# First attention sets loaded during the projection, and the norm sums one step later

## The reference, cut to what matters

```python
h = _layernorm(x, axis=-1) * (1 + ca) + sa
q = rmsnorm(proj(wq_w, wq_b), qn_w)
k = rmsnorm(proj(wk_w, wk_b), kn_w)
v = proj(wv_w, wv_b)
allowed = (i[None, :] <= i[:, None]) & (i[:, None] - i[None, :] < WINDOW)
scores = jnp.einsum('bhqd,bhkd->bhqk', q, k) * scale
attn = jax.nn.softmax(jnp.where(allowed[None, None], scores, -jnp.inf), axis=-1)
out = jnp.einsum('bhqk,bhkd->bhqd', attn, v)
...
def _wn(v, g):                 # the experts' weight norm: a sum of squares over each row
    n = jnp.sqrt(jnp.sum(v * v, axis=-1, keepdims=True))
    return v / jnp.maximum(n, EPS) * g[:, None]
```

## Time and profile before

| what | value |
|---|---|
| median of 3 runs | 2500.89 us (2485.25 to 2501.75) |
| profiled execution, its own time | 2496.8 us |
| its span | 2494.9 us |
| PE busy | 1932.4 us, 77% |
| DVE busy | 1669.4 us, 67% |
| ACT busy | 1089.1 us, 44% |
| POOL busy | 820.3 us, 33% |
| mean granted clock | 0.87 |
| DMA of SP's and ACT's queues | 205.50 MB, 33% of 16 engines' span |

### The profile page before, as it was taken

The page is one execution under the profiler, slowest core; times in us unless marked ns, Lnnn a source line. Parts: engine busy times, 40 slices in busy tenths (PEclk is TensorE's granted clock), DMA queues, the critical chain, the costliest instruction groups (busy, mean ns, idle before and its releaser), DMA issues. The chain is left out here.

```text
span 2494.9 us, 46728 instructions
## 1 busy us (share of the span) xinstructions
PE 1932.4 (77%) x15652; PEld 1349.0 (54%) x15652; DVE 1669.4 (67%) x3311; ACT 1089.1 (44%) x2227; POOL 820.3 (33%) x692
## 2 busy tenths in 40 slices
PE   5994888976638999998199599999998724289991
PEld 2773666755537899987054233333333523177771
DVE  3664566646778666665589587888774577765555
ACT  2772444443526333332166066666566344232222
POOL 1454333430234333332067211111111033356650
PEclk8996999987559999999599599999999855599996
DMA  4337988822336211111535824444420101242226
GB/s 142 127 138 159 183 161 169 171 67 86 129 108 191 91 52 48 48 52 35 201 138 180 147 45 69 69 69 69 69 36 2 30 32 64 94 125 84 82 77 223
DMA packets 176821, 253.47 MB, mean 102 GB/s; under 512 B 29380, under 2 KB 118500, under 8 KB 174564
## 3 DMA queue, kind: packets, MB, share of 16 engines
q1 hardware_dynamic: 157124, 205.50, 33.0%
q0 software_dynamic: 14976, 40.91, 5.3%
q10 hardware_dynamic: 4512, 4.24, 0.5%
HBM read 170.59 MB, written 79.21 MB: 100 GB/s over the span
## 5 line engine op out<-in xcount | busy, mean ns | idle before, releaser
L848 DVE TENSOR_REDUCE a_mx<-a_pmx 128x1 f32<-128x512 f32 (+5 forms) x928 | 506.0, 589 | 184.9 <-PE a_pmx L714 80.9
L912 ACT ACTIVATE a_probs<-a_pst 128x512 f32<-128x512 f32 (+2 forms) x864 | 426.0, 552 | 359.4 <-PE a_pst L732 194.9
L709 PE MATMUL a_pmx<-a_Ks,a_Qs 96*128 96x192 bf16 (+4 forms) x1280 | 344.9, 309 | 64.0 <-DMA a_V<-v_d 62.7
L1841 PE MATMUL m_ph<-m_zh,m_w 128*128 128x256 f16 x2808 | 327.9, 277 | 37.5 <-DVE m_w L1216 18.3
L1841 PEld LDWEIGHTS m_ph<-m_zh,m_w 128*128 x2808 | 274.0, 99 | 86.0 <-issue 50.1
L1857 PE MATMUL m_py<-m_w,m_zh 128*128 x2808 | 319.2, 273 | 0.6 <-DVE m_free L1907 0.4
L732 PE MATMUL a_pst<-a_Qs,a_Ks 99*128 99x192 bf16 (+5 forms) x1344 | 306.8, 291 | 9.3 <-ACT a_probs L912 6.1
L1857 PEld LDWEIGHTS m_py<-m_w,m_zh 128*128 128x128 f16 x2808 | 271.0, 98 | 32.0 <-issue 1.3
L1887 ACT ACTIVATE x_res<-m_ph,m_b,m_s 128x256 f32<-128x256 f32 x312 | 159.2, 561 | 247.3 <-PE m_ph L1841 239.3
L709 PEld LDWEIGHTS a_pmx<-a_Ks,a_Qs 96*128 96x128 bf16 x1280 | 125.1, 100 | 238.2 <-DVE a_mx L848 128.1
L1794 POOL DMA_INDIRECT m_zh<-z_d,m_src x156 | 171.2, 1098 | 225.5 <-PE m_pt L1824 182.9
(11 more groups left out here) (281 smaller groups left out, 3260.7 us busy)
## 6 DMA issues: line engine op xcount, KB each, us to landing
parts_d<-p_part SPq DMA_DIRECT2D x64, 384.0 KB, 3.2
a_Qs<-parts_d SPq DMA_DIRECT2D x192, 128.0 KB, 4.5
a_Ks<-parts_d SPq DMA_DIRECT2D x192, 128.0 KB, 7.2
v_d<-p_vt SPq DMA_DIRECT2D x16, 1024.0 KB, 4.4
a_V<-v_d SPq DMA_DIRECT2D x32, 512.0 KB, 9.1
m_got<-y_d SPq DMA_DIRECT2D x32, 512.0 KB, 6.6
a_wst<-L_w1T SPq DMA_DIRECT2D x16, 512.0 KB, 6.4
a_wst<-L_w2T SPq DMA_DIRECT2D x16, 512.0 KB, 4.9
```

Source lines behind the costliest of these rows:

```text
L709: mm = nc.tensor.matmul(pmx[:, buf, o:o + cols], Qs[par][0:KROWS, h, i * P:(i + 1) * P], Ks[par][0:KROWS, h, k0:k1], start=True, stop=not ...
L848: nc.vector.tensor_reduce(mx[:, part, hs[0]:hs[0] + len(hs), i], src, AX.X, ALU.max).then_inc(m_done, 1)
L912: nc.scalar.activation(probs[:, (hg * NV + v) % 2, hs[0]:hs[0] + len(hs), q0:q1], src, ACT.Exp, scale=HD ** -0.5).then_inc(exp_done, 1)
L1841: mm = nc.tensor.matmul(ph[:, (G * par + g) % 4, q * ROWS:(q + 1) * ROWS], self.w1[:, bass.ds(e, 1), c, wp, m * P:(m + 1) * P].rearrange(" ...
```

## The change

The 4 sets and their semaphores are made before project, so that SP can load the sets 0, 1 and 2 in slots k = 1, 3 and 5 of the projection's last batch, each after that slot's own store, in both layers. The loads at the start of attend go. In attend SP issues load_weights ahead of send_max instead of behind it. DVE's turn of expert e moves from step 2e + 1 to step 2e + 2, ahead of the same score units 3 and 6; that of the last expert goes to step 15, ahead of score units 11 and 13 of 15. POOL waits for its own four memsets before it goes on.

```diff
                     with ExitStack() as hold:
+                        self.Ks, self.Qs, self.V4 = sets("Ks", ...), sets("Qs", ...), sets("V4", ...)
+                        self.kq_in = [self.sem(hold, f"{T}kq_in{i}") for i in range(SETS)]
+                        self.project(layer)
                         self.attend(layer)
...
+            EARLY = (1, 3, 5)
...
                             sp.dma_start(pd[:, q % QK, :, ...], part[:, q % 4, :, :]).then_inc(part_out[q % 4], 16)
+                        if isinstance(b, int) and b == B - 1 and k in EARLY:
+                            if k == EARLY[0]:
+                                for half in range(2):
+                                    sp.wait_ge(v_out[half], 16)
+                                for i in range(4):
+                                    sp.wait_ge(part_out[i], 16 * 2)
+                            self.load_set(sp, layer, EARLY.index(k), 0, EARLY.index(k))
...
+            turn_at = {("st", 2 * e + 2, a): (e, a // 6) for e in range(EXPERTS - 1) for a in (3, 6)}
+            turn_at.update({("st", STEPS - 1, NE - 4): (EXPERTS - 1, 0), ("st", STEPS - 1, NE - 2): (EXPERTS - 1, 1)})
...
-                    if NORM and s % 2 and kind == "st" and a in (3, 6):
-                        dve_turn(dve, s // 2, a // 6)
+                    if NORM and (kind, s, a) in turn_at:
+                        dve_turn(dve, *turn_at[kind, s, a])
...
                         pool.memset(Ks[i][KROWS:KAUG, :, :], 1.0).then_inc(ones_set, 1)
+                    pool.wait_ge(ones_set, SETS)
...
-                    for hg in range(SETS - 1):
-                        if hg > 0:
-                            sp.wait_ge(kq_in[hg - 1], 16 * loads)
-                        load(sp, hg, 0, hg)
...
-                            send_max(sp, (hg + 1) % SETS, s + 1)
                             if NORM:
                                 load_weights(sp, 2 * b + hg // 2, hg % 2, s)
+                            send_max(sp, (hg + 1) % SETS, s + 1)
...
                     for s in range(STEPS - SETS, STEPS):
+                        if NORM:
+                            load_weights(sp, s // 2, s % 2, s)
                         if s < STEPS - 1:
                             send_max(sp, (s + 1) % SETS, s + 1)
-                        if NORM:
-                            load_weights(sp, s // 2, s % 2, s)
```

More of the change, by code:

```diff
@@ L38 @@
 HALF = 512
+SETS = 4
+LOADS = 2 * SLOTS + 1
+SLOT_Q, SLOT_K = (0, 0, 0, 1, 1, 2), (0, 1, 2, 0, 1, 0)
 HT = HALF // P
@@ L104, in build @@
             for layer in range(LAYERS):
-                self.project(layer)
                 with ExitStack() as scales:
@@ L110, in build @@
                     with ExitStack() as hold:
+                        T = f"a{layer}_"
+                        sets = lambda n, shape, t: [self.sb(hold, f"{T}{n}{i}", shape, t) for i in range(SETS)]
+                        self.Ks, self.Qs, self.V4 = sets("Ks", [KAUG, HG, L], BF16), sets("Qs", [KAUG, HG, L], BF16), sets("V4", [P, TPB, HG, 2 * HD], F32)
+                        self.kq_in = [self.sem(hold, f"{T}kq_in{i}") for i in range(SETS)]
+                        self.project(layer)
                         self.attn = self.sb(hold, f"attn{layer}", [P, TILES, D])
@@ L612, in key_blocks, with load_set @@
         return out
+    def load_set(self, sp, layer, par, b, hg):
+        pd = self.parts_d[layer]
+        row = lambda base: bass.ds(hg * (HG * HD) + base, HG * HD)
+        for dst, base, slots in ((self.Qs[par], 0, SLOT_Q), (self.Ks[par], D, SLOT_K)):
+            for s, part in enumerate(slots):
+                src = pd[part, row(base), bass.ds(b * L, L)].rearrange("(g e) n -> e g n", e=HD)
+                sp.dma_start(dst[s * HD:(s + 1) * HD, :, :], src).then_inc(self.kq_in[par], 16)
+        vsrc = self.v_d[layer][bass.ds(b * L, L), bass.ds(hg * (HG * 2 * HD), HG * 2 * HD)].rearrange("(t p) n -> p t n", p=P)
+        sp.dma_start(self.V4[par][:, :, :, :].rearrange("p t h e -> p t (h e)"), vsrc).then_inc(self.kq_in[par], 16)
     def attend(self, layer):
@@ L617, in attend @@
             T = f"a{layer}_"
-            SETS = 4
             sb = lambda n, s, t=F32: self.sb(ctx, T + n, s, t)
             sem = lambda n: self.sem(ctx, T + n)
-            Ks = [sb(f"Ks{i}", [KAUG, HG, L], BF16) for i in range(SETS)]
-            Qs = [sb(f"Qs{i}", [KAUG, HG, L], BF16) for i in range(SETS)]
-            V4 = [sb(f"V4{i}", [P, TPB, HG, 2 * HD]) for i in range(SETS)]
+            Ks, Qs, V4, kq_in = self.Ks, self.Qs, self.V4, self.kq_in
             probs = sb("probs", [P, 2, HG, HALF])
@@ L637, in attend @@
             ones_set = sem("ones_set")
-            kq_in = [sem(f"kq_in{i}") for i in range(SETS)]
             max_in = [sem(f"max_in{i}") for i in range(SETS)]
@@ L671, in attend @@
             mask = self.causal if layer else self.window
[L672 to L684, removed]
+            loads = LOADS
+            load = lambda sp, par, b, hg: self.load_set(sp, layer, par, b, hg)
             def load_weights(sp, e, second, s):
```

## The result

The changed kernel takes 2530.08 us (median of 4 runs, 2522.53 to 2535.56), the kernel before 2497.99 us (4 runs): the ratio is 1.0135, with a 95% interval of 1.0089 to 1.0182. It is slower by 32 us, where 2492 us was forecast and 2512 us was the end of the range. The profiled execution after took 2528.51 us, its span 2526.6 us, against 2496.8 and 2494.9.

The account below looks back on a forecast made before the run. It saw waits for loads at both attention starts (40.5 us) and DVE's wait for POOL as the prize; -8 + 4 - 4 + 1.5 = -6.5 us against 2496.8 gave 2490, named as 2492, range 2460 to 2512.

Parts of the forecast that it names:

- Layer 0's start, -8: Layer 0's projection and attention start: waits go (-26.0), step 0 gives back 1.9, projection 16 us longer; net -8 us.
- rival 1: Queue gaps swallow the early loads: projections end only 7 and 12 us later, steps take 17.2 us; 2458 us, chance 0.2.
- Layer 1, +4: Layer 1's projection and attention: start saves 14.5 and small DMAs 2.6 us, projection 21 us longer; net +4 us.
- the stores' wait: Projections' last batch: stores behind a set land up to 12 us late and ACT waits for them, stopping the pipeline.
- What the steps of layer 0 give, -4: Layer 0's attention steps 1 to 13: a period of 18.4 us, 238 us against 242.1; -4 us.
- the turn is hidden in DVE's slack: Layer 0's attention steps: the turn's 2.8 us of DVE cost nothing; only DVE's wait for POOL costs.
- the place in the queue: Layer 0's attention steps: small DMAs go behind 1 MB of weights and land late, odd and even steps alike, period 18.4 us.
- The bound of +1: Slow bound for layer 0's attention steps: +1 us if the period is 18.8 us.
- Rival 3: Early loads as forecast, but weights ahead of send_max take the turn's gain, 18.8 us a step; 2495 us, chance 0.15.
- The end, +1.5: End of layer 0's attention: last turn, POOL's square and adds finish 1.5 us later (0 to 4).
- The clock rule: Layer 0's projection stretch: bursts alternating with DMA waits drop TensorE to 1.2 GHz after each stall; part of rival 2.
- rival 2: ACT's store stalls add up and TensorE's clock falls: projections 24 and 26 us longer, 18.8 us a step; 2509 us, chance 0.15.

Follow-up runs that it names:

- e5: e1 with POOL, after the turn, also waiting until that step's split is through before its second square of W2: 2482.83 us, ratio 0.9940.
- e1: Kernel before with only the turns moved to step 2e + 2; send_max stays ahead of the weights, no early loads: 2496.27 us, ratio 1.0004.
- e15: Changed kernel whole, with W2 loaded in rows of 4 KB instead of 1 KB: 2527.64 us, ratio 1.0117.
- e4: Changed kernel with send_max put back ahead of load_weights (turns moved and early loads kept): 2495.82 us, ratio 1.0000.
- e6: Changed kernel without early loads, weights ahead of send_max in even steps only (W1): 2502.61 us, ratio 1.0019.
- e7: Changed kernel without early loads, weights ahead of send_max in odd steps only (W2): 2535.65 us, ratio 1.0147.
- e13: e7 with W2's 512 KB a DMA in rows of 4 KB instead of 1 KB: 2521.03 us, ratio 1.0092.
- e12: e7 with each W2 DMA bringing 128 KB in 128 rows of 1 KB, norm sums incomplete: 2496.04 us, ratio 0.9996.
- e14: e7 with each W2 DMA bringing 128 KB in 512 rows of 256 bytes, norm sums incomplete: 2499.15 us, ratio 1.0012.

## Why the prediction was wrong

**Layer 0's start, -8: right.** Measured -7.8. The projection was 18.1 us longer (16 forecast), with waits of ACT for stores of 6.4, 5.2 and 8.6 us as described, and step 0 was in its place. The queue did keep its order and the gaps did not swallow three sets in a row, so rival 1 fell; the 7 and 12 us at which it put the projections came from no row.

**Layer 1, +4: right, a little short.** The projection was 23.1 us longer (21), and the attention 563.6 - 546.1 = 17.5 us shorter (17.1): +5.5 us. I had given the stores' wait as its only cause; SP's own issues, held for 8.3 us, are a second one that the sum did not have.

**What the steps of layer 0 give, -4: wrong, and this is the step that failed.** It said that all steps would have a period of 18.4 us, 12 x 18.4 + 17.2 = 238. They took 274.4. Over the 223.9 us that e5 shows to be the floor, my working had one term, +14. The runs show three:

- the turn beside the split, +15.8 (e1 against e5). I wrote that the turn is hidden in DVE's slack, which holds for its 2.8 us (e5's steps take 17.22 us with the turn in them). But I moved it without asking what it releases: POOL's square and adds, which until then ran after the split and now run in it. DVE's wait for POOL did go, as forecast (20.6 us over the attention before, none after); what came instead was nearly as dear.
- the small DMAs behind the weights' bytes, +24.0 (e15's 263.7 against e1's 239.7; against e4, which has the early loads as e15 has, +22.7). This is the mechanism that I had, the place in the queue. It was mis-sized and misplaced: I gave it to odd and even steps alike, and nearly all of it is in odd steps, where the wait for sq_done parts nothing (e6 against e7). In even steps the small DMAs of the changed kernel land within 3.2 us of their issue, in the odd steps 1 to 11 after 8.9 to 9.7.
- SP's held issue, +10.8 (after against e15, in the steps; the medians of these two kernels differ by 2.4 us only, those of e7 and e13 by 14.6). My model took the rows of the issues as fixed durations. The row of 3.27 us for six DMAs in the earlier trace rows, where others had 2.7, was a sign that they are not.

Part of the last two terms is TensorE's clock, which the sum left out. The changed kernel's 13 steps are 33.4 us longer than e4's. TensorE's six waits for the small DMAs in them are 20.7 us, and the same 2821 matmuls keep it busy 14.8 us longer (235.2 against 220.4), at a mean granted clock of 0.91 against 0.97.

The bound of +1 came from a period of 18.8, that is, from the same model with a slightly larger number. It bounded the number and not the model, so the range could not hold the result. Rival 3, weights ahead of send_max taking the turn's gain, was the right kind of case, and its price was too low: 18.8 instead of 17.2 us a step is 19 us over the 12 steps, 5 more than the forecast's 14, and the runs show 33 to 35 (33.4 after against e4; 24.0 + 10.8).

**The end, +1.5: too low.** From step 14's mark to the output projection 29.7 us became 35.1: +5.4. POOL's chain behind DVE's last turn ends the block as said (its last add at 572.23), but steps 14 and 15 took 16.2 and 13.4 us, 13.3 and 11.4 before. The runs part it: with the turns moved and send_max first the same stretch takes 32.7 us (e1, e4), so the turns are 3.0 of it, of which POOL beside the split is 2.1 (e5: 30.6), and the weights ahead are the other 2.4. These are single traces; e7, e12, e13 and e14, with the turns moved and the weights of even steps behind, lie between 31.2 and 33.8.

**The clock rule** stands beside rival 2. The granted clock fell in both places: in layer 0's old window from 0.88 to 0.82, and in the steps, after TensorE's waits, where it cost the time above. The rival's end, 2509, was 21 us short: its projections, 24 and 26 us longer, were dearer than the 18.1 and 23.1 measured, and its steps were priced at 18.8 us, where they took 21.1.

Sum with measured terms: -7.8 + 5.5 + 32.3 + 5.4 - 1.0 - 0.3 - 2.5 = +31.6 us.

## What to carry to other kernels

Before a small, urgent DMA is put behind bulk transfers on one queue, ask two things of the trace: how many bytes stand ahead of it, and in how many pieces, since the first delays its landing and the second the issue itself and all that the issuing engine does next. When work of one engine is moved, look at what it releases on the others, and what runs beside it at the new place: the moved 2.8 us cost nothing, the POOL operations behind them 16 us. Loads moved into a busy block are paid for if they come as a lump: one set, two DMAs a slot between the stores, made layer 0's projection 1.3 us longer, the same set in one slot 6.0, and three sets 18.1.

## What the runs showed of the hardware

An 8 KB DMA mostly takes SP 0.5 to 0.6 us to issue, but 4.1 to 5.5 us when it comes right behind a set and two weight DMAs of 512 rows each, whether a row has 1 KB (after, e7) or 256 bytes (e14); with 128 rows (e12), or the same bytes in rows of 4 KB (e13), it takes 1.6 us at most. I had known only its place in the queue. How many pieces the queue holds, the runs do not tell.

A subtraction on DVE of 32 x 128 with both sources in SBUF takes 0.28 us, and 2.46 beside POOL's 128 x 1024 operations; a cast from SBUF to SBUF 0.21 and 0.86. In the changed kernel's first attention every cast and subtraction that was held so ended within 0.15 us of the end of a POOL operation. The cast and the subtraction just ahead of them, which read PSUM, took 0.27 and 0.28 us beside POOL's square, as in the kernel before.
